# Sums of h moved from GpSimd to the vector engine, and down products two gaps later, in a two-layer attention and feed-forward kernel

## The chip, the cores and the metric

The kernel runs on one core of a Trainium2 chip. TensorE multiplies matrices, VectorE (DVE) and ScalarE (ACT) do elementwise work, GpSimd (POOL) does elementwise work and issues some of the transfers, SyncE (SP) issues the others. Each engine takes its instructions in program order; semaphores tie the engines together. The metric is the device time of the whole program in microseconds, median of several runs. Lower is better.

## What is computed

The input `x` is 16 x 128 x 1024 in f32. The first layer adds to it a cross attention of its layer norm with a context. The second layer, where nearly all the time goes, is a feed-forward block on int4 weights with a scale and a zero for each group of 64:

```
x = x + _L0_xattn_ref(_layernorm(x), ctx_1024, Wq, Wk, Wv, Wskip)
x = x + _L0_ffn_ref(_layernorm(x), ...)
# _L0_ffn_ref:
g = einsum('bsh,ih->bsi', x, Wg);  u = einsum('bsh,ih->bsi', x, Wu)   # 2048 tokens, 1024 -> 2752
h = silu(g) * u
return einsum('bsi,hi->bsh', h, Wd)                                  # 2752 -> 1024
```

Every weight is `(nibble - zero) * scale`.

## The kernel before

**Precision.** f32 data is split in two 16-bit parts, a rounded "hi" (a cast on ACT) and the residual "lo" (a subtraction on DVE). Each product of two blocks is three matmuls: hi·hi, hi·lo, lo·hi.

**Fewer products.** Gate/up and down are each a product of 2 x 2 blocks, done with seven block products instead of eight (the Winograd form of Strassen's scheme). That needs sums of blocks of the weights (S1 to S4), of x (T1 to T4) and, in the down product, of h.

**Tiles.** The 2752 inner features go in 10 pairs (PAIRS) of 256 and a remainder. For each pair there are four `instance`s, one for each half of the pair's features (e = 0, 1) and each half of the tokens (g = 0, 1). Here they are called A (e 0, g 0), B (e 1, g 0), C (e 0, g 1) and D (e 1, g 1). An instance is seven products of 12 matmuls (L569). Their outputs are assembled on DVE in this order: `u1_out`, `u2_out`, `c22_out`, `c21_out`, `c12_out`; ACT does `m1_copy` after the first product, `silu0` after the third, `silu1` after `c12_out`; DVE forms h in `h0_out` (after `c21_out`) and `h1_out` (after `silu1`).

**Groups.** The h of A and B is one group (number 2p for pair p), that of C and D the next (2p+1). Seven blocks of h go into the down product: A11 and A12 (h0 of the first and second instance), A22 (h1 of the second), and four sums, S3 = A11 - A21, S2 = A22 - S3, S1 = A21 + A22, S4 = A12 - S2 (in the code `S3H` etc.). Before the change all four are made on GpSimd: S3 by `last_sum` (L400), S2, S1 and S4 by `first_sums` (L407, L408, L411), one after the other. Each block is then rounded on ACT (`h_block_hi`, L915) and its residual made on DVE (`h_block_lo`, L1396).

**Gaps.** The down product of a group has ten pieces, `down_gap(1)` to `down_gap(10)` (matmuls L607 to L609). TensorE does them in the gaps between the seven products of the two instances that follow: gap 1 after the second product of the first one, gap 2 after the third, and so on to gap 6 after the seventh; gaps 7 to 10 after the first four products of the next. So group 2p-1 is multiplied during A and B of pair p, and group 2p during C and D. Gap 1 needs A11 and A12, and gap 2 begins with a product of S2 and one of S1. ACT scales the results out of PSUM (L918), DVE adds to them (L1399), and GpSimd adds them to `out` in HBM with accumulating transfers: `add11` (L416), `add12` (L422) and `add2` (L429).

**What TensorE waits for in an instance.** The third product needs `m1_copy`; the fourth needs `u1_out` (L1359); the sixth `u2_out` (L1364); the seventh `c22_out`. On DVE `u1_out` stands behind the residuals of S2 and S1.

**Weights.** DVE makes the weights of the next instances in the same stream, in slots `work(0)` to `work(6)` between the steps above: a job is `job_nibbles` (L1249, L1250), `job_minus` (L1254, twice), `times_scale` twice (L1259), residuals (L1264) and sums. A job of gate/up stands in A and B's end for the next e, a job of down weights in B and C. `quant`, `raw` and `grid` are single buffers, so each job's transfers start when the last one is done with them.

**The order of work** is written out by hand in `even_tile` (A and C) and `odd_tile` (B and D), once for ACT and once for DVE. A loop runs over pairs 1 to 9 (here: nine turns); pair 0 stands ahead of it, the last group's down product and the remainder behind it.

## Time and profile before

| | us |
|---|---|
| median of 3 runs | 1476.07 (1474.54 to 1476.49) |
| the profiled execution | 1475.23 |
| its span, first to last instruction | 1473.4 |
| TensorE busy | 1414.7 |
| VectorE busy | 1119.2 |
| ScalarE busy | 678.6 |
| GpSimd busy | 421.3 |

Matmuls overlap in the pipeline: a 128 x 512 one is listed with 0.38 us, but in an unbroken row the next begins 0.216 us later. A row of 12 has 2.75 us in the list, and what follows begins 2.59 us after its start. Where a wait stands in square brackets behind a matmul, the time lost against an unbroken row is that wait and 0.16 to 0.17 us more. VectorE's records overlap a little too: a 128 x 512 operation is listed with 0.68 us, and an independent one can begin 0.60 us after its start, a dependent one 0.72.

### The profile page before, as it was taken

Reading aid. Unit: us, or ns where it says so; the run is one execution under the profiler, and the core shown is the slowest. Engines: PE = TensorE matmul, PEld = TensorE weight load, DVE = VectorE, ACT = ScalarE, POOL = GpSimd, SP = SyncE. Lnnn points to the kernel's source line nnn. Section 1 sums busy time; section 2 is a strip of 40 time slices with the busy share of each in tenths; the row PEclk is TensorE's granted clock in tenths of the full one; section 3 lists DMA queues with packets and bytes.
Section 4 is the critical chain, followed back from the end, with each engine's and each line's share of the span. In section 5 each row is a group of like instructions: output and inputs, shape, how many; then the busy total and the mean of one; then the engine's idle time right before and its main releaser. Section 6 shows DMA issues by size and latency. Waiting matters only on the chain.

```text
span 1473.4 us, 19706 instructions
## 1 busy us (share of the span) xinstructions
PE 1414.7 (96%) x6534; PEld 690.0 (47%) x6534; DVE 1119.2 (76%) x1535; ACT 678.6 (46%) x1269; POOL 421.3 (29%) x425
## 2 busy tenths in 40 slices
PE   8999999899999999999999999999999999999988
PEld 6677764344444444444444444444444444444433
DVE  5898977777778778778778778777778778778565
ACT  6889883334434434444443443443443444444320
POOL 1242322223223323332323323332233233233200
PEclk9999999999999999999999999999999999999999
DMA  5322222276575585675675665764765755756694
GB/s 165 114 85 92 83 86 57 58 143 110 101 146 102 104 142 97 117 125 102 122 121 102 132 121 95 132 117 91 142 113 98 139 107 105 122 115 121 114 322 186
DMA packets 58552, 174.86 MB, mean 119 GB/s; under 512 B 7952, under 2 KB 10768, under 8 KB 54160
## 3 DMA queue, kind: packets, MB, share of 16 engines
q0 software_dynamic: 34560, 83.90, 36.8%
q1 hardware_dynamic: 23808, 90.20, 20.5%
q8 instruction: 20, 0.33, 0.1%
q10 hardware_dynamic: 144, 0.26, 0.1%
q14 instruction: 20, 0.16, 0.0%
HBM read 73.67 MB, written 100.66 MB: 118 GB/s over the span
## 4 chain that ended last, share of the span: by engine, by line
PE 70%; DVE 10%; issue 10%; POOL 5%; ACT 4%; DMA 0%; SPq 0%; DVEq 0%; POOLq 0%
PE ps L569 35%; PE ps L607 8%; PE ps L609 7%; PE ps L608 7%; DVE park L1396 3%; POOL temps L407 3%; PE ps L531 3%; PE ps L498 3%; POOL temps L408 2%; PE ps L756 2%; PE ps L486 1%; PE ps L526 1%; PE ps L520 1%; DVE park L1264 1%; DVE temps L1373 1%
## 5 line engine op out<-in xcount | busy, mean ns | idle before, releaser
L569 PE MATMUL ps<-xt,w_gu 128*128 128x512 f16 x3528 | 798.3, 380 | 2.1 <-DVE temps L1373 2.1
L569 PEld LDWEIGHTS ps<-xt,w_gu 128*128 128x128 f16 x3528 | 345.3, 98 | 420.0 <-DVE temps L1359 5.4
L918 ACT ACTIVATE stage<-ps,pow 128x512 f32<-128x512 f32 x300 | 204.1, 686 | 307.9 <-PE ps L609 306.3
L1399 DVE SCALAR_TENSOR_TENSOR stage<-ps,pow,stage 128x512 f32<-128x512 f32 x220 | 159.5, 747 | 156.0 <-ACT stage L918 87.3
L607 PE MATMUL ps<-park 128*128 128x512 f16 x560 | 212.8, 380 | 35.7 <-DVE park L1396 35.7
L609 PE MATMUL ps<-park 128*128 128x512 f16 x560 | 212.6, 380 | 0.0
L608 PE MATMUL ps<-park 128*128 128x512 f16 x560 | 212.5, 379 | 0.0
L429 POOL DMA_DIRECT2D out<-stage x80 | 69.4, 867 | 288.8 <-ACT stage L918 288.8
L416 POOL DMA_DIRECT2D out<-stage x80 | 70.6, 883 | 276.0 <-DVE stage L1399 276.0
L1396 DVE TENSOR_TENSOR park<-temps,park 128x512 bf16<-128x512 f32 x140 | 125.7, 909 | 20.9 <-ACT park L915 18.1
L915 ACT CAST park<-temps 128x512 f16<-128x512 f32 x140 | 84.2, 615 | 124.2 <-DVE temps L1383 69.9
L607 PEld LDWEIGHTS ps<-park 128*128 128x128 f16 x560 | 54.7, 98 | 116.6 <-DVE park L1396 28.1
L407 POOL TENSOR_TENSOR temps<-temps 128x512 f32<-128x512 f32 x20 | 43.6, 2180 | 217.4 <-DVE temps L1389 217.4
L609 PEld LDWEIGHTS ps<-park 128*128 128x128 bf16 x560 | 54.8, 98 | 66.3 <-issue 0.3
L608 PEld LDWEIGHTS ps<-park 128*128 128x128 f16 x560 | 54.8, 98 | 61.4
L422 POOL DMA_DIRECT2D out<-stage x60 | 68.4, 1140 | 12.1 <-DVE stage L1399 12.1
L498 PE MATMUL ps<-w_gu,park 128*128 128x256 f32 x256 | 62.4, 388 | 1.1 <-ACT w_gu L779 0.5
L794 ACT ACTIVATE temps<-ps,neg_max 128x256 f32<-128x256 f32 x128 | 59.3, 486 | 7.8 <-DVE neg_max L1185 7.5
L531 PE MATMUL ps<-temps,w_gu 128*128 128x512 f32 x128 | 60.2, 593 | 0.6 <-ACT temps L789 0.6
L808 ACT ACTIVATE temps<-temps,inv_total 128x256 f32<-128x256 f32 x128 | 54.7, 504 | 6.9 <-DVE inv_total L1200 6.9
L498 PEld LDWEIGHTS ps<-w_gu,park 128*128 128x128 f32 x256 | 47.6, 193 | 11.7 <-issue 5.3
L1264 DVE TENSOR_TENSOR w_gu<-raw,w_gu 128x1024 f16<-128x1024 f32 (+1 forms) x43 | 53.0, 1232 | 0.0
(123 smaller groups left out, 1715.4 us busy)
## 6 DMA issues: line engine op xcount, KB each, us to landing
out<-stage POOLq DMA_DIRECT2D x80, 512.0 KB, 5.4
out<-stage POOLq DMA_DIRECT2D x140, 256.0 KB, 4.5
grid<-grids SPq DMA_DIRECT2D x136, 256.0 KB, 5.2
raw<-packed SPq DMA_DIRECT2D x34, 512.0 KB, 4.3
out<-stage SPq DMA_DIRECT2D x17, 512.0 KB, 2.7
stage<-x SPq DMA_DIRECT2D x13, 512.0 KB, 3.7
xt<-out SPq DMA_DIRECT2D x12, 512.0 KB, 12.3
out<-xt SPq DMA_DIRECT2D x12, 512.0 KB, 2.7
```

What stands on the lines that cost most here:

```text
L407: pool.tensor_tensor(s3h, u1[:, 1, :], s3h, ALU.subtract).then_inc(s_h_sum, 1)
L416: pool.dma_start(out[t, :, 0:NOUT], stage[:, d % 2, 0:NOUT], accum_op=ALU.add).then_inc(s_add11[d % 2], 16)
L498: mm = pe.matmul(ps_e[f][:, t, :], xn[b % XNS][:, cols], kk[:, par, :], start=True, stop=True)
L531: mm = pe.matmul(ps_o, v_t[:, par, h, :], prob_t[:, f, h, :], start=False, stop=(h == 1))
L569: mm = pe.matmul(bank, w_gu[e][:, wp, w, P * j:P * j + P], xt[:, xb, xp, j, cols], start=(fresh and n == 0), stop=(n == 3 * J - 1), skip_g ...
L607: pe.matmul(bank, h_hi[:, h, rows], w_d[:, 0, w, :], start=fresh, stop=False, skip_group_check=not fresh)
L608: pe.matmul(bank, h_hi[:, h, rows], w_d[:, 1, w, :], start=False, stop=False, skip_group_check=not fresh)
L609: return pe.matmul(bank, h_lo[:, h, rows], w_d[:, 0, w, :], start=False, stop=True, skip_group_check=not fresh)
L915: act.copy(h_hi[:, block, :], src).then_inc(s_h_hi, 1)
L918: return act.activation(dst, ps[:, bank, :], ACT.Copy, scale=pow2[:, 10:11])
L1396: dve.tensor_tensor(h_lo[:, block, :], src, h_hi[:, block, :], ALU.subtract).then_inc(s_h_lo, 1)
L1399: return dve.scalar_tensor_tensor(out=part, in0=ps[:, bank, :], scalar=pow2[:, 10:11], in1=part, op0=ALU.mult, op1=ALU.add)
```

## The change

Four things are changed together.

1. S3, S2 and S4 are made on DVE (`last_sum`, `first_sums_of_h`, `fourth_sum`). S1 stays on GpSimd (`fourth_block`) with a semaphore of its own, and now waits for `h1_out` alone. DVE waits for it ahead of `u1_out`.
2. The down products of the first group of a pair (2p, multiplied during C and D) are shifted by two gaps (`LATER = 2`): gaps 1 to 4 lie after products 4 to 7 of C, gaps 5 to 10 after products 1 to 6 of D. Those of the other group stay.
3. The four C12 parts of a group rotate over three places, so that the next group begins with another place than the last one ended with.
4. Weight work is moved between slots: `times_scale` of `raw` in A goes behind `u1_out`; the last two down weight sums go from B to C, and the residuals of the mixed down weights stand later in C; nibbles and zeros of the next jobs one slot earlier in D and one later in C. On ACT, S4 is rounded after `silu0`.

```diff
+LATER = 2
...
-        part12 = [stage[:, 0, NOUT:N], stage[:, 1, NOUT:N], more[:, :], stage[:, 0, NOUT:N]]
+        places = [stage[:, 0, NOUT:N], stage[:, 1, NOUT:N], more[:, :]]
+        part12 = [[places[(g + k) % 3] for k in range(QUADS)] for g in range(2)]
...
-            def first_sums(group):
-
-                n = 4 * (group // 2) + 2 * (group % 2) + 1
-                pool.wait_ge(s_h1, n + 1)
-                pool.wait_ge(s_h_lo, 7 * group + S3H + 1)
-                pool.tensor_tensor(s3h, u1[:, 1, :], s3h, ALU.subtract).then_inc(s_h_sum, 1)
-                pool.tensor_tensor(s1h, u1[:, 0, :], u1[:, 1, :], ALU.add).then_inc(s_h_sum, 1)
-                pool.wait_ge(s_h_sum, 4 * group + 2)
-                pool.wait_ge(s_h_lo, 7 * group + A12 + 1)
-                pool.tensor_tensor(act_h[:, 1, :], act_h[:, 1, :], s3h, ALU.subtract).then_inc(s_h_sum, 1)
...
+            def fourth_block(group):
+
+                pool.wait_ge(s_h1, 2 * group + 2)
+                wait(pool, s_h_lo, 7 * (group - 1) + S1H + 1)
+                pool.tensor_tensor(s1h, u1[:, 0, :], u1[:, 1, :], ALU.add).then_inc(s_h_sum1, 1)
...
-                instance(4 * p + 2, 0, 1, 0, first_gaps(2 * p, 12 * p + 8))
-                instance(4 * p + 3, 1, 1, 0, last_gaps(2 * p))
+                instance(4 * p + 2, 0, 1, 0, first_gaps(2 * p, LATER, 12 * p + 8))
+                instance(4 * p + 3, 1, 1, 0, last_gaps(2 * p, LATER))
...
+            def last_sum(group):
+
+                dve.wait_ge(s_h1, 2 * group + 1)
+                wait(dve, s_h_lo, 7 * (group - 1) + S2H + 1)
+                dve.tensor_tensor(s3h, act_h[:, 0, :], u1[:, 0, :], ALU.subtract).then_inc(s_h_sum, 1)
+
+            def first_sums_of_h(group):
+
+                dve.wait_ge(s_h1, 2 * group + 2)
+                dve.wait_ge(s_h_lo, 7 * group + S3H + 1)
+                dve.tensor_tensor(s3h, u1[:, 1, :], s3h, ALU.subtract).then_inc(s_h_sum, 1)
+
+            def fourth_sum(group):
+
+                dve.wait_ge(s_h_sum, 3 * group + 2)
+                dve.wait_ge(s_h_lo, 7 * group + A12 + 1)
+                dve.tensor_tensor(act_h[:, 1, :], act_h[:, 1, :], s3h, ALU.subtract).then_inc(s_h_sum, 1)
...
                 before()
+                if group is not None:
+                    first_sums_of_h(group)
                 work(0)
                 if group is not None:
                     h_block_lo(group, S2H)
                     h_block_lo(group, S1H)
+                    dve.wait_ge(s_h_sum1, group + 1)
                 u1_out(n, 0, sums)
```

TensorE, from the last three products of B on, before the change (L569 is an instance's product, L607 to L609 a down product):

```order
L569 MATMUL ps<-xt,w_gu 128x512 x60
...
L607 MATMUL ps<-park 128x512
L608 MATMUL ps<-park 128x512
L609 MATMUL ps<-park 128x512
...
L569 MATMUL ps<-xt,w_gu 128x512 x12
```

and with the change:

```order
L556 MATMUL ps<-xt,w_gu 128x512 x60
L574 REGISTER_ALU
L556 MATMUL ps<-xt,w_gu 128x512 x24
...
L594 MATMUL ps<-park 128x512
L595 MATMUL ps<-park 128x512
L596 MATMUL ps<-park 128x512
```

Before, three products of B and two of C stood in a row (60 matmuls), then gap 1, then one product; now three of B and four of C stand in a row (84), then gap 1.

VectorE at the beginning of the loop, which is the beginning of A, before (L1389 is `h1_out`, L1259 `times_scale`, L1396 the residuals of S2 and S1):

```order
L1389 SCALAR_TENSOR_TENSOR temps<-temps,pow 128x512
...
L1259 SCALAR_TENSOR_TENSOR quant<-quant,pow,grid 128x1024
...
L1259 SCALAR_TENSOR_TENSOR raw<-raw,pow,grid 128x1024
...
L1396 TENSOR_TENSOR park<-temps,park 128x512
```

and with the change (L1414 is `h1_out`, L1458 the sum S2, L1280 `times_scale`, L1421 the residuals, L1384 `u1_out`):

```order
L1414 SCALAR_TENSOR_TENSOR temps<-temps,pow 128x512
...
L1458 TENSOR_TENSOR temps<-temps 128x512
...
L1280 SCALAR_TENSOR_TENSOR quant<-quant,pow,grid 128x1024
...
L1421 TENSOR_TENSOR park<-temps,park 128x512
...
L1384 TENSOR_TENSOR temps<-ps,temps 128x512
```

The sum S2 stands directly behind `h1_out`, and one `times_scale` instead of two stands ahead of the residuals.

VectorE at the end of B, before (L1264 the residuals of the plain down weights, L1297 to L1304 the four down weight sums, L1373 `c21_out`):

```order
L1264 TENSOR_TENSOR park<-raw,park 128x1024
L1297 TENSOR_TENSOR quant<-quant 128x512
L1299 TENSOR_TENSOR quant<-raw,quant 128x512
L1302 TENSOR_TENSOR raw<-raw,quant 128x512
...
L1304 TENSOR_TENSOR raw<-raw 128x512
L1373 TENSOR_TENSOR temps<-ps,temps 128x512
```

and with the change (L1285, L1398 `c21_out`, L1408 `h0_out`, L1319 and L1321 the first two sums, L1402 `c12_out`):

```order
L1285 TENSOR_TENSOR park<-raw,park 128x1024
L1398 TENSOR_TENSOR temps<-ps,temps 128x512
L1408 SCALAR_TENSOR_TENSOR temps<-temps,pow 128x512
...
L1421 TENSOR_TENSOR park<-temps,park 128x512
L1319 TENSOR_TENSOR quant<-quant 128x512
L1321 TENSOR_TENSOR quant<-raw,quant 128x512
L1402 TENSOR_TENSOR temps<-ps,temps 128x512
```

`c21_out` no longer stands behind four sums, and two of them stand between it and `c12_out`; the other two are in C.

## Rows read from the trace of the kernel before

**Rows 1.** The page: span, busy time and share, instructions of each engine.
```profile
span 1473.4 us, 19706 instructions
PE 1414.7 (96%) x6534; PEld 690.0 (47%) x6534; DVE 1119.2 (76%) x1535; ACT 678.6 (46%) x1269; POOL 421.3 (29%) x425
```
**Rows 2.** TensorE's waits, whole span: who waited for whom, us, times, longest.
```profile
PE ps L607 <- DVE park L1396: 35.7, 40, 1.8
PE ps L569 <- DVE temps L1373: 2.1, 1, 2.1
```
**Rows 3.** The same for the nine loop turns alone, 327 to 1345 us.
```profile
PE ps L607 <- DVE park L1396: 31.6, 36, 1.8
```
**Rows 4.** TensorE in time, around gap 2 of A: start, duration, [idle before].
```profile
771.51 13.11 PE L569 MATMUL ps<-xt,w_gu 128*128 128x512 f16 x60
785.76 2.75 PE L569 MATMUL ps<-xt,w_gu 128*128 128x512 f16 x12
790.20 0.39 PE L607 MATMUL ps<-park 128*128 128x512 f16 x1 [1.68 <-DVE park L1396]
791.80 0.39 PE L607 MATMUL ps<-park 128*128 128x512 f16 x1 [0.78 <-DVE park L1396]
```
**Rows 5.** TensorE in time, around gap 2 of C.
```profile
828.72 13.11 PE L569 MATMUL ps<-xt,w_gu 128*128 128x512 f16 x60
846.04 0.39 PE L607 MATMUL ps<-park 128*128 128x512 f16 x1 [0.33 <-DVE park L1396]
847.55 0.39 PE L607 MATMUL ps<-park 128*128 128x512 f16 x1 [0.69 <-DVE park L1396]
```
**Rows 6.** VectorE and GpSimd in time, beginning of A.
```profile
783.11 1.22 DVE L1254 TENSOR_TENSOR raw<-raw,grid 128x1024 f32<-128x1024 int32 x1
784.91 1.28 DVE L1259 SCALAR_TENSOR_TENSOR quant<-quant,pow,grid 128x1024 f32<-128x1024 f32 x1
785.08 2.23 POOL L407 TENSOR_TENSOR temps<-temps 128x512 f32<-128x512 f32 x1 [9.94 <-DVE temps L1389]
786.11 2.29 DVE L1259 SCALAR_TENSOR_TENSOR raw<-raw,pow,grid 128x1024 f32<-128x1024 f32 x1
787.28 2.23 POOL L408 TENSOR_TENSOR temps<-temps 128x512 f32<-128x512 f32 x1
788.32 1.75 DVE L1396 TENSOR_TENSOR park<-temps,park 128x512 bf16<-128x512 f32 x1
```
**Rows 7.** VectorE, GpSimd and ScalarE in time, end of B and beginning of C.
```profile
833.85 0.69 DVE L1297 TENSOR_TENSOR quant<-quant 128x512 f32<-128x512 f32 x1
838.69 0.68 DVE L1377 TENSOR_TENSOR temps<-ps,temps 128x512 f32<-128x512 f32 x1
839.41 0.72 ACT L898 ACTIVATE temps<-temps,pow 128x512 f32<-128x512 f32 x1 [0.59 <-DVE temps L1377]
841.02 0.75 DVE L1389 SCALAR_TENSOR_TENSOR temps<-temps,pow 128x512 f32<-128x512 f32 x1
844.01 1.26 POOL L408 TENSOR_TENSOR temps<-temps 128x512 f32<-128x512 f32 x1
844.07 0.62 ACT L915 CAST park<-temps 128x512 f16<-128x512 f32 x1 [0.78 <-POOL temps L407]
847.41 0.68 DVE L1359 TENSOR_TENSOR temps<-ps,temps 128x512 f32<-128x512 f32 x1
```
**Rows 8.** Busy time of each engine in one loop turn: stretch, length, PE, PEld, DVE, ACT, POOL, clock.
```profile
779.20:892.30 113.10, 109.62 (x507) 49.02 (x505) 86.92 (x108) 47.24 (x70) 35.09 (x32) 1.00 0.64 116
```
**Rows 9.** TensorE in time, first pair: gap 2 of the first group.
```profile
281.21 0.61 PE L607 MATMUL ps<-park 128*128 128x512 f16 x1 [0.85 <-DVE park L1396]
282.47 3.71 PE L569 MATMUL ps<-xt,w_gu 128*128 128x512 f16 x12
```
**Rows 10.** Line L297, the load of `raw`: issue to landing, all 34.
```profile
DMA to landing us min/median/max: 3.1/4.3/6.7
```
**Rows 11.** TensorE in time, the loop's one product at a lower clock.
```profile
1018.44 4.36 PE L569 MATMUL ps<-xt,w_gu 128*128 128x512 f16 x12
```

312 lines of the change are left out of this document (173 added, 139 removed).

## The prediction

> **What bounds the kernel now.** First the page: TensorE is busy for 1414.7 of 1473.4 us [rows 1], so nothing can be won but its pauses, unless matmuls are removed, and none is. Then its waits: 35.7 us stand in 40 waits at one line, L607, the down products, for the residuals of h (L1396) [rows 2]; 36 of these waits, 31.6 us, are in the nine loop turns [rows 3]. Then the timeline of one turn: all four waits stand in gap 2, ahead of the product of S2 and that of S1, two in A and two in C [rows 4, 5]. A row of 60 matmuls takes 60 x 0.216 = 12.95 us, a row of twelve 2.59. In A, the product at 785.76 ends a row at 788.35, and the next matmul starts at 790.20: 1.85 us lost, where the view says 1.68. A wait costs 0.17 more than it is listed with. The nine turns lose 31.6 + 36 x 0.17 = 37.7 us, about 2.8 in each A and 1.35 in each C.
>
> Why is gap 2 late in A? GpSimd's sum S2 (L407) and VectorE's `times_scale` alternate: L407 takes 2.23, the second `times_scale` 2.29 where the first took 1.28, L408 2.23, and the residual of S2 1.75 instead of 0.68 [rows 6]. With VectorE idle GpSimd needs 1.26 for the same sum [rows 7]. Each of them waits for the other to end. The Trainium skill says the same of it ("SBUF — State Buffer", section "Who interferes with whom"): a VectorE instruction with two SBUF inputs and a GpSimd instruction that reads SBUF exclude one another, and the first to issue holds the port for the whole instruction. By that rule the trace agrees: 1.26 us of work took up to 2.23.
>
> **The change, part by part.** *C, the shifted group.* I follow the new order with the durations of the rows, on the clock of [rows 5, 7]. B's seventh product ends at 828.72 + 36 x 0.216 = 836.49; call this T. Gap 2 of C now lies after the fifth product, at T + 14.2 (five products of 2.59 and gap 1 of 6 x 0.216), and the residuals of S2 and S1, which came at T + 9.4 and T + 10.9 [rows 5], are far ahead of it. These two waits go: 1.35 a turn. But gaps 1 and 2 covered something: the fourth product waits for `u1_out`, which stands behind both residuals. It used to be wanted at T + 10.36, and now, with no gap ahead of it, at T + 7.77. So what is late next is `u1_out`, and the chain to it has to be walked.
> - VectorE is free at 833.85, where the four down weight sums began [rows 7]. `c21_out` takes their place at 834.10 (the sixth product ends at 833.90, and a result is read 0.2 later), then `h0_out`, the residual of S3 and two sums: 0.72 + 0.67 + 0.60 + 0.72 + 0.61, so `c12_out` starts at 837.42, T + 0.9. It was 838.69 [rows 7].
> - ScalarE rounds the first mixed down weights from 837.53, 0.95 us, then `silu1` 838.48 to 839.20 (0.72 [rows 7]). `h1_out` 839.23 to 839.97. It was 841.02.
> - Sum S2 on VectorE, priced by L1297 of the same shape, 0.69 [rows 7]: to 840.67. GpSimd sees `h1_out` 0.09 later, so it finds the port taken and does S1 from 840.67 to 841.93, at its 1.26. ScalarE rounds S2 (0.62) to 841.32 and S1 to 842.59; the residual of S2 waits for GpSimd and ends at 842.5, that of S1 at 843.28.
> - `u1_out` follows 0.60 after the start of that residual, 843.20 to 843.88, and TensorE starts 0.13 later (788.32 + 1.75 to 790.20 [rows 4, 6]): 844.01. It is wanted at 844.26. Slack 0.25 us.
>
> That is thin. The loop's two-register waits on VectorE and ScalarE may cost 0.05 to 0.1 each in such a chain, so the new wait lies between 0 and 0.4 us; I take 0.1, since the walk ends ahead of time: +1.0 in nine turns.
>
> *A, the group that stays.* D's end is T'. VectorE there: `nibbles` now before `c21_out`, then `h0_out`, residual S3, an add, two `job_minus` of 1.13 (listed 1.22 [rows 6]), so `c12_out` at T' + 1.3; `silu1` to T' + 2.8, `h1_out` to 3.6, sum S2 to 4.3. In between, what stood ahead of `h1_out`, 2.3 us of `job_minus`, is gone. GpSimd's S1 runs 4.3 to 5.55, `times_scale` waits and runs to 6.65. ScalarE first scales gap 1's result, ready at T' + 5.83, until 6.6, then rounds S2 to 7.2; residual 8.0, seen at 8.1. It is wanted at 9.07. S1: 8.7 against 9.72. `u1_out`: 9.3 against 10.36. All two waits go, 2.8 us a turn, with 1 us to spare.
>
> *What else moves.* VectorE gains three sums a group, 6 x 0.69 = 4.1 us a turn, on 86.9 of 113.1 [rows 8]: 91 of 109, still 84%. They cost nothing as long as nobody waits behind them: in A the fourth sum and the `times_scale` moved behind `u1_out` delay `u2_out` to T' + 15.9, wanted at 20.1. In C two down weight sums, their residuals and the fourth sum end at T + 13; mixed down weights are wanted at 14.2, `u2_out` (13.5) at 15.5. GpSimd loses 3 of 4 sums, and its transfers, which stand behind the sums, start no later. The C12 places: each is written again at least three parts later; even at 7 us a transfer the place is free; nothing. Rounding S4 after `silu0`: S4 is wanted in gap 4; nothing.
>
> *The load of `raw` in C* is the other narrow place. It can be issued at T + 13.1, and VectorE waits for it in `nibbles`, ahead of `c21_out`, `h0_out` and the add whose result the last product of gap 4 needs at T + 24.6. With the median landing of 4.3 [rows 10] that add ends at T + 23.2: slack 1.35 us, so landings up to 5.65 cost nothing.
>
> *Outside the loop.* There are 35.7 - 31.6 = 4.1 us in four waits, 0.7 more by their 0.17, 2.3 for the first C's wait for `c21_out` (2.1 [rows 2]), and 1.6 at half clock behind the first one (3.71 against 2.75, 0.61 against 0.38 and the five matmuls between [rows 9]): 8.7. `c21_out` loses the four sums ahead of it, 2.8 us, so its wait goes. But the first pair's VectorE runs late, and without gap 1 as cover `m1_copy` and `u1_out` hold TensorE there for some 1.5 + 1.65 us. Won: 8.7 - 3.2 = 5.5, between 3 and 8.7.
>
> *The clock.* The other product at a lower clock (4.36 against 2.75 [rows 11]) stands right behind the two waits of an A. With these gone I take its 1.6 us as gone.
>
> **Sum.** -37.7 + 1.0 - 5.5 - 1.6 = -43.8 us. The profiled execution took 1475.2, 0.8 under the median: 1476.1 - 43.8 = 1432.3, say 1432.5. If every pause named here vanished: 37.7 + 8.7 + 1.6 = 48, 1428.
>
> **The rivals.**
> - *GpSimd first.* S1 on GpSimd and S2 on VectorE are released by the same `h1_out`. If GpSimd takes the port first, the sum starts 1.26 later, `u1_out` in C is seen at 844.6 instead of 844.0, and TensorE waits 0.35 us; with late registers up to 1.2. In nine turns +3 to +11, less the 1.0 already in the sum: 1435 to 1443. Against it: `h1_out` to the next VectorE operation is 0, to GpSimd 0.09 (841.02 + 0.75, and [rows 6] has L407 at 785.08). The skill's SBUF page (section "SBUF: two separate sides") has the rule that whoever starts first holds the port for the whole instruction; by it this rival's wait is the whole 1.26 or nothing. Chance 20%.
> - *The raw load lands late.* The longest seen is 6.7 [rows 10]: 1.05 us a turn, +9: 1442. Against it: in C it is issued before GpSimd's first transfer of the group. 6%.
> - *The chain in C stays as long as it is.* From the start of `h1_out` to the end of `u1_out` 841.02 to 848.09 [rows 7], 7.07 us. Then `u1_out` is seen at 846.4, 2.2 late, +19: 1451. 8%.
> - *A's waits stay in part* (S2 ready, but held behind something on ScalarE): half of 25 us stays, 1445 to 1458. 5%.
> - *Slower.* The `raw` load in C, 512 KB, would have to land more than 5.65 + 4.2 = 9.9 us after its issue: then the new wait is larger than the 4.15 us that a turn gains. At 12 us a turn loses 2.1, nine lose 19, and with the 6 won outside it ends at 1489. No landing over 6.7 is in the trace, but VectorE's stream is fuller than before and other transfers move under it. 3%.
> - *Nothing gained*: the waits only change their line, 1476. 2%.
>
> **How the numbers follow.** The forecast (1428 to 1436) has 56%, GpSimd first 20%, late load 6%: these give 1428 to 1443. To have 8 in 10 with some room for the chain in C, the range is 1427 to 1447. Within 0.2% (3 us, about what a measurement of this kernel can tell from no change) 3%, slower 4%, faster 93%.
>
> **What would show it.** Right: no wait at a down product in A or C beyond the first pair; the period of a turn 108.9 to 109.3 us instead of 113.1; VectorE's S2 sum ending about 0.7 after `h1_out`, GpSimd's S1 at 1.3 to 2.0. Wrong at the chain in C: a wait of an L556 product on `u1_out` in every C. Wrong at the load: `nibbles` in C waiting for the transfer over 3 us and a down product waiting for L1424. Wrong at the lock: VectorE's sum listed with about 1.9 us.

## The result, and the profile after

| | median us | ratio to before | 95% interval |
|---|---|---|---|
| before | 1476.28 (1474.54 to 1476.49, 4 runs) | | |
| after | 1425.69 (1425.62 to 1425.75, 4 runs) | 0.966 | 0.9643 to 0.9677 |

The change gains 50.6 us. The forecast was 43.8, and its range (1427 to 1447) begins 1.3 us above the result: the direction came as told, the size did not. The waits that were named went, but not all for the reasons given, as the experiments show. The profiled execution of after took 1425.65 us, span 1423.8, so between the two profiled executions there are 49.6 us.

The page of after, span and TensorE, answers to [rows 1]:

```profile
span 1423.8 us, 19828 instructions
PE 1402.8 (99%) x6534; PEld 692.5 (49%) x6534; DVE 1121.7 (79%) x1595; ACT 682.3 (48%) x1269; POOL 312.8 (22%) x365
```

TensorE's waits over the whole span, those outside the attention part (who waited <- for whom: us, times, longest), answer to [rows 2]:

```profile
PE ps L507 <- DVE xt L1211: 4.2, 4, 1.8
PE ps L556 <- DVE temps L1384: 1.4, 1, 1.4
PE ps L556 <- ACT temps L874: 1.3, 1, 1.3
PE ps L743 <- DVE xt L1736: 1.2, 2, 1.0
```

The 40 waits at the down products, 35.7 us, are gone: L594, the first matmul of a down product (L607 before), has no row here. The two L556 rows are in C of the first pair; L507 are transposes, 3.7 of the 4.2 us in A and B of the first pair; L743 is in the remainder behind the loop.

One loop turn of after (stretch, length, busy time and instructions of PE, PEld, DVE, ACT, POOL, granted clock, DMA share, GB/s) answers to [rows 8]:

```profile
1023.64:1132.42 108.78, 108.78 (x506) 49.31 (x504) 87.20 (x114) 47.66 (x71) 24.14 (x26) 1.00 0.66 121
```

A turn is 108.78 us instead of 113.10, and TensorE is busy for all of it. VectorE works 87.20 us in it, where 86.92 were before, although three sums a group were added. Those are 4.1 us, but VectorE's other instructions are held up less by GpSimd's sums: a residual of h (L1421, L1396 before) is listed with 709 ns on average instead of 909, 2.8 us for the 14 of a turn. GpSimd falls from 35.09 to 24.14.

The chain in C, in the turn whose T (end of B's seventh product, start of C's first) is 1140.03: VectorE, GpSimd and ScalarE in time (start, duration), which answer to [rows 7]:

```profile
1140.97 0.69 DVE L1402 TENSOR_TENSOR temps<-ps,temps 128x512 f32<-128x512 f32 x1
1142.79 0.75 DVE L1414 SCALAR_TENSOR_TENSOR temps<-temps,pow 128x512 f32<-128x512 f32 x1 [0.54 <-ACT temps L884]
1143.57 0.69 DVE L1458 TENSOR_TENSOR temps<-temps 128x512 f32<-128x512 f32 x1
1143.62 1.76 POOL L431 TENSOR_TENSOR temps<-temps 128x512 f32<-128x512 f32 x1 [8.73 <-DVE temps L1414]
1145.42 1.14 ACT L904 CAST park<-temps 128x512 f16<-128x512 f32 x2 [0.51 <-POOL temps L431]
1144.95 1.82 DVE L1421 TENSOR_TENSOR park<-temps,park 128x512 bf16<-128x512 f32 x2 [0.68 <-ACT park L904]
1146.68 0.68 DVE L1384 TENSOR_TENSOR temps<-ps,temps 128x512 f32<-128x512 f32 x1
```

`c12_out` starts at T + 0.94 (forecast 0.9), `h1_out` at T + 2.76, the sum S2 (L1458) takes 0.69, and GpSimd's S1 (L431), released by the same `h1_out`, starts 0.05 behind it, is listed with 1.76 and ends at T + 5.35. `u1_out` (L1384) ends at T + 7.33. With the 0.13 of a semaphore TensorE could go on at T + 7.46, and it wants to at T + 7.77: 0.31 us of room. The forecast had 0.25.

In A the two sums come in the other order. Here is the A behind that C, whose start T' is 1194.42:

```profile
1197.20 0.75 DVE L1414 SCALAR_TENSOR_TENSOR temps<-temps,pow 128x512 f32<-128x512 f32 x1 [0.19 <-ACT temps L884]
1198.08 1.76 DVE L1458 TENSOR_TENSOR temps<-temps 128x512 f32<-128x512 f32 x1
1198.04 1.26 POOL L431 TENSOR_TENSOR temps<-temps 128x512 f32<-128x512 f32 x1 [3.23 <-DVE temps L1414]
```

GpSimd starts 0.04 us ahead, and VectorE's sum is listed with 1.76 instead of 0.69. It is so in A of all nine loop turns; in the other eleven of the 20 groups VectorE is first. A has room for it: no TensorE wait follows.

**Where the 49.6 us are.** Split the program where the 84 matmuls of the remainder start. Before they start at 1402.14, after at 1357.59: 44.55 us are won up to there. Of these 39.5 are in the nine loop turns (1018.5 us before, 979.0 after, by the starts of TensorE's matmuls), 3.3 ahead of the loop and 1.8 between the loop and the remainder. From the remainder's first matmul to the end of the span it was 71.25 us and is 66.26: another 5.0 us, in a part whose order of work the diff leaves as it was. The forecast of 43.8 is nearly exact for the first part, and had nothing for the second. The experiments begin there.

### The profile page after: what moved, and what is told of

The parts are those of the page before. It is cut to its first block, busy times and chain, and to the rows that moved or that the text cites. A ratio compares the mean times of both kernels' runs of the same rounds, so it can differ in the third digit from the quotient of the medians.

```text
span 1423.8 us, 19828 instructions
## 1 busy us (share of the span) xinstructions
PE 1402.8 (99%) x6534; PEld 692.5 (49%) x6534; DVE 1121.7 (79%) x1595; ACT 682.3 (48%) x1269; POOL 312.8 (22%) x365
## 4 chain that ended last, share of the span: by engine, by line
PE 89%; DVE 5%; ACT 3%; issue 2%; DMA 0%; POOL 0%; SPq 0%; DVEq 0%; POOLq 0%; ACTq 0%
PE ps L556 50%; PE ps L596 8%; PE ps L595 8%; PE ps L594 8%; PE ps L518 3%; PE ps L485 3%; PE ps L743 2%; PE ps L473 1%; PE ps L513 1%; PE ps L507 1%; ACT temps L781 1%; ACT temps L795 1%; PE ps L723 1%; DVE neg_max L1206 0%; DVE w_gu L1285 0%
## 5 line engine op out<-in xcount | busy, mean ns | idle before, releaser
L556 PE MATMUL ps<-xt,w_gu 128*128 128x512 f16 x3528 | 795.9, 379 | 2.7 <-DVE temps L1384 1.4
L556 PEld LDWEIGHTS ps<-xt,w_gu 128*128 128x128 f16 x3528 | 345.1, 98 | 417.9 <-DVE temps L1384 1.9
L594 PE MATMUL ps<-park 128*128 128x512 f16 x560 | 212.2, 379 | 0.0
L904 ACT CAST park<-temps 128x512 f16<-128x512 f32 x140 | 83.1, 614 | 64.8 <-DVE temps L1408 38.1
L1421 DVE TENSOR_TENSOR park<-temps,park 128x512 bf16<-128x512 f32 x140 | 98.4, 709 | 17.0 <-ACT park L904 13.9
L595 PEld LDWEIGHTS ps<-park 128*128 128x128 f16 x560 | 54.8, 98 | 66.1
L594 PEld LDWEIGHTS ps<-park 128*128 128x128 f16 x560 | 54.8, 98 | 66.1
L596 PEld LDWEIGHTS ps<-park 128*128 128x128 bf16 x560 | 54.8, 98 | 66.1
L408 POOL DMA_DIRECT2D out<-stage x60 | 66.9, 1115 | 6.6 <-DVE stage L1424 6.3
L431 POOL TENSOR_TENSOR temps<-temps 128x512 f32<-128x512 f32 x20 | 30.7, 1535 | 150.0 <-DVE temps L1414 150.0
L1285 DVE TENSOR_TENSOR w_gu<-raw,w_gu 128x1024 f16<-128x1024 f32 (+1 forms) x43 | 53.1, 1235 | 7.7 <-ACT w_gu L844 6.1
```

Source lines behind the costliest of these rows:

```text
L556: mm = pe.matmul(bank, w_gu[e][:, wp, w, P * j:P * j + P], xt[:, xb, xp, j, cols], start=(fresh and n == 0), stop=(n == 3 * J - 1), skip_g ...
L594: pe.matmul(bank, h_hi[:, h, rows], w_d[:, 0, w, :], start=fresh, stop=False, skip_group_check=not fresh)
L595: pe.matmul(bank, h_hi[:, h, rows], w_d[:, 1, w, :], start=False, stop=False, skip_group_check=not fresh)
L596: return pe.matmul(bank, h_lo[:, h, rows], w_d[:, 0, w, :], start=False, stop=True, skip_group_check=not fresh)
L904: act.copy(h_hi[:, block, :], src).then_inc(s_h_hi, 1)
L1421: dve.tensor_tensor(h_lo[:, block, :], src, h_hi[:, block, :], ALU.subtract).then_inc(s_h_lo, 1)
```

## The experiments

The second column is the median. The other three are of the profiled execution: the nine loop turns, the start of the remainder's first matmul, and the time from there to the end of the span.

| kernel | us | nine turns | start of the remainder | remainder |
|---|---|---|---|---|
| before | 1476.3 | 1018.5 | 1402.1 | 71.3 |
| `x_act5`: before + 5 small ScalarE copies | 1470.12 | 1018.3 | 1400.6 | 66.9 |
| `x_dve5`: before + 5 small VectorE memsets | 1478.85 | 1020.3 | 1402.8 | 73.3 |
| `x_sums`: before + sums on VectorE | 1453.61 | 1005.8 | 1385.5 | 66.0 |
| `y_pool`: after, sums on GpSimd | 1444.92 | 989.9 | 1369.9 | 72.5 |
| `y_pool_act5`: that + 5 ScalarE copies | 1439.35 | 989.9 | 1371.2 | 66.0 |
| `y_order`: after, old order of the down weights | 1463.37 | 1013.3 | 1397.2 | 66.2 |
| `y_late1`: after, shift of one gap | 1467.06 | 1014.3 | 1399.7 | 66.1 |
| `y_scale`: after, both scales ahead of `u1_out` in A | 1425.53 | 979.0 | 1357.6 | 66.1 |
| `y_dup2`: after, 1.2 us more ahead of `u1_out` in C | 1434.74 | 987.1 | 1368.9 | 65.4 |
| `y_s1dve`: after, S1 on VectorE too | 1424.53 | 979.0 | 1357.3 | 65.4 |
| `y_first2`: after, first pair reordered | 1424.60 | 979.0 | 1357.5 | 66.4 |
| `y_best`: both, and more of the first pair | 1421.01 | 979.0 | 1353.4 | 66.0 |
| after | 1425.69 | 979.0 | 1357.6 | 66.3 |

### Five instructions that do nothing

In the remainder of before, ScalarE and TensorE in time. `y_silu` is L1099; in square brackets stands the idle time before the instruction and what ended it:

```profile
1420.03 0.62 ACT L1106 CAST park<-temps 64x512 f16<-64x512 f32 x1
1424.59 0.68 ACT L1099 ACTIVATE temps<-ps,pow 64x512 f32<-64x512 f32 x1 [3.94 <-issue]
1426.89 0.82 PE L756 MATMUL ps<-park,w_gu 128*128 128x512 f16 x3 [4.30 <-DVE xt L1678]
1428.10 1.49 PE L756 MATMUL ps<-park,w_gu 128*128 128x512 f16 x3
```

"issue" says that ScalarE waited for no semaphore. Behind it stands the longest wait of TensorE outside the attention part, 4.30 us, and then matmuls at a lower granted clock (a row of three takes 1.49 instead of 0.82). The same place in after:

```profile
1376.11 0.62 ACT L1127 CAST park<-temps 64x512 f16<-64x512 f32 x1
1376.63 0.68 ACT L1120 ACTIVATE temps<-ps,pow 64x512 f32<-64x512 f32 x1
1379.07 0.82 PE L743 MATMUL ps<-park,w_gu 128*128 128x512 f16 x3 [1.03 <-DVE xt L1736]
```

The third `y_silu` follows at once, TensorE waits 3.27 us less, and no slow matmuls come behind. Counted by the records of the trace, with the loop's body counted once, the third `y_silu` is ScalarE's 832nd of 840 before and the 838th of 846 after, since the rearranged gaps write a few more. (The recorded expectation below counts otherwise, and has 626 and 630.) So the first theory is that a place in ScalarE's instruction stream pauses, not a piece of work. `x_act5` is before with

```
+            for k in range(5):
+                act.copy(total[:, k // 4, k % 4:k % 4 + 1], pow2[:, k:k + 1])
             act.wait_ge(s_down3, 2 * QUADS * PAIRS)
             act.wait_ge(s_weight, 6 * PAIRS + 5)
```

> The kernel before with five one-column ScalarE copies (into unused columns of `total`) added in the remainder, at a place where ScalarE waits 5.78 us anyway, and nothing else. What is tested: in the kernel before, ScalarE stands 3.94 us with no releaser ahead of the third `y_silu` (instruction 626 of its program, counting each copy of a row that order prints as xN), TensorE then waits 4.30 us at 1426.89, and in the kernel after both are gone (the same instruction is number 630 there). Theory A (the pause belongs to a place in ScalarE's instruction stream, where new instructions are fetched, on a DMA queue that row loads fill at that moment): the pause moves to another instruction, up to five earlier in the remainder's work, TensorE's wait of 4.30 shrinks to about 1, and the time falls by 3 to 5 us, to 1471 to 1473; if it lands on a copy that feeds the y chain earlier, a smaller wait of its own is left. Theory B (the pause belongs to the moment or to what the third `y_silu` waits for, such as a semaphore from VectorE or the loads of the rows): it stays at the third `y_silu`, with TensorE's 4.3 us, and the time stays within 1 us of 1476.3.

1470.12 us (1469.32 to 1471.83) against 1476.35 on the same chip, ratio 0.9956 (0.9939 to 0.9972): 6.2 us faster through five instructions that compute nothing, 0.9 us more than the expected range allowed. ScalarE and TensorE in its remainder:

```profile
1412.22 0.62 ACT L1107 CAST park<-temps 64x512 f16<-64x512 f32 x1 [5.01 <-DVE temps L1636]
1420.25 0.68 ACT L1101 ACTIVATE temps<-ps,pow 64x512 f32<-64x512 f32 x1
1422.68 0.82 PE L756 MATMUL ps<-park,w_gu 128*128 128x512 f16 x3 [1.59 <-DVE xt L1680]
```

The pause is gone from the third `y_silu`, TensorE's wait is 1.59 us instead of 4.30, and the matmuls behind run at full clock. The DMA view tells where the pause went. It lists packets of a queue q14 of kind "instruction" (packets, MB, share of 16 engines); first before, in 1420.7 to 1424.6, ScalarE's pause:

```profile
q14 instruction: 1, 0.01, 0.5%
```

then `x_act5`, in 1407.0 to 1412.2, where ScalarE waits 5.01 us for VectorE in any case:

```profile
q14 instruction: 2, 0.02, 0.8%
```

The packet in the pause starts at 1422.94, and another follows 4.83 us later; the two of `x_act5` start at 1407.02 and 1411.84, 4.82 apart. The view doesn't say for which engine a packet is, so that these are ScalarE's is read from their places and distances, not shown. The remainder is 4.4 us shorter; the other 1.5 to 1.8 us of the 6.2 lie ahead of it, within the spread of before (1474.3 to 1479.6), and I do not assign them.

`x_dve5` is the control: the same number of instructions, on VectorE.

```
+            for k in range(5):
+                dve.memset(inv_total[:, k // 4, k % 4:k % 4 + 1], 0.0)
             dve.memset(park[HALF:P, 1792:2816], 0.0)
```

> The kernel before with five one-column VectorE memsets (into unused columns of `inv_total`) added in the remainder, ahead of the memset of `park`, and nothing else; ScalarE's program is untouched. Theory A (a place in ScalarE's own stream): ScalarE's 3.94 us ahead of the third `y_silu` stay, TensorE waits 4.3 us, time 1476 within 1 us. Theory A' (two engines' fetches collide on one queue, VectorE's at about 1420.5 and ScalarE's at 1423): moving VectorE's by five instructions parts them, the pause falls to about half, the time by about 2 us. Theory B (the moment, not the stream): as A.

1478.85 (10 runs), ratio 1.0015 (1.0005 to 1.0025): 2.5 us slower. ScalarE's pause stays at its third `y_silu`, at 3.94 us to the digit:

```profile
1427.62 0.68 ACT L1099 ACTIVATE temps<-ps,pow 64x512 f32<-64x512 f32 x1 [3.94 <-issue]
1416.13 0.69 DVE L1628 TENSOR_TENSOR w_gu<-temps,w_gu 128x512 bf16<-128x512 f32 x1 [1.93 <-issue]
```

That "no change" was expected and not found has its reason in the second row: VectorE now has a pause of its own, 1.93 us, and it stands in the chain of `y`: TensorE waits 5.9 us there instead of 4.3. A q14 packet starts at 1414.21, with the pause; before, the one in its place starts at 1415.44, while VectorE works. So five instructions moved VectorE's pause into the chain and left ScalarE's alone. The theory of colliding fetches falls: ScalarE's pause did not shrink.

The same was tried once more on another kernel, `y_pool` (below), which has the pause (3.85 us) and TensorE's wait (4.60):

> The kernel after with the three sums back on GpSimd, and the five one-column ScalarE copies in the remainder as well. Alone, the sums on GpSimd gave 1444.9 and a pause of ScalarE of 3.85 us ahead of the third `y_silu`, with TensorE's wait of 4.6 us behind it, as in the kernel before. Theory A (a place in ScalarE's stream): the pause leaves that spot here too, 1438.5 to 1441. Theory B (what the remainder's timing is): 1444.9 within 1 us.

1439.35 (1437.36 to 1442.77) instead of 1444.92, the remainder 6.4 us shorter, and TensorE's wait there:

```profile
1392.45 0.82 PE L761 MATMUL ps<-park,w_gu 128*128 128x512 f16 x3 [0.78 <-DVE xt L1730]
```

Over all kernels: the three whose ScalarE program has 840 records (before, `x_dve5`, `y_pool`) pause at the third `y_silu`, 3.85 to 3.94 us; the eleven with 845 or 846 don't. That the diff made this stream six records longer is therefore the reading that fits all fourteen kernels; `x_act5`, which changes nothing else, wins 4.4 of the 5.0 us. VectorE's stream is 30 records longer by the same count, and in after it pauses 3.75 us ahead of the last `u2_out`, where nobody waits for it.

The Trainium skill ("Runtime: NRT & Kernel Launch", section "Instruction fetch mechanics") has the mechanism: each engine's stream is fetched block by block over a DMA queue while the block before is executed, strictly in sequence, a branch out of the loaded blocks stalls, and crossing a block's border is "mostly hidden". The trace agrees with a border at a place in the stream and differs in the last point: behind the loop the pause was not hidden, with 3.2 to 4.1 us. That a border between blocks, and not the way out of the loop, is what costs here is not shown. Pauses of nearly one length stand beside different loads of the DMA engines: 3.94 us (ScalarE) in before with a DMA share of 1.02 in 1420.6 to 1424.6, 3.75 us (VectorE) in after with 0.55 in 1347.6 to 1351.4.

### Sums alone, and all the rest alone

`x_sums` is before with the three sums of after on VectorE, and S1 alone on GpSimd:

```
             def even_tile(n, group, before, sums, work):
                 before()
+                first_sums_of_h(group)
                 work(0)
                 ...
                 u1_out(n, 0, sums)
                 down_gap(group, 1)
+                fourth_sum(group)
             def odd_tile(n, group, own, before, sums, work):
                 ...
                 down_gap(group, 7)
+                last_sum(own)
                 work(0)
```

`y_pool` is the counterpart, after with GpSimd's `last_sum` and `first_sums` of before put back and VectorE's taken out (GpSimd's part):

```
             for group in range(2 * PAIRS):
-                fourth_block(group)
-                for at in range(1, 11):
+                first_sums(group)
+                cut = 8 if group % 2 else 6
+                for at in range(1, cut):
                     adds(group, at)
+                if group + 1 < 2 * PAIRS:
+                    last_sum(group + 1)
+                for at in range(cut, 11):
+                    adds(group, at)
```

> The kernel before with only the three sums (S3, S2, S4) moved from GpSimd to VectorE; down products, places of C12 and weights work stay as they were. My theory (the down products in C start before their inputs are there, so the shift by two gaps is what removes most of the wait; the sums themselves only shorten the chain): after h1_out VectorE makes the S2 sum in 0.69 us instead of GpSimd's 1.26 to 2.2, and GpSimd starts S1 at the same moment, so that the chain to `u1_out` is about 1.3 us shorter in C and in A, and the waits fall by about that: 1.3 us in A and in C in each of the nine turns, 20 to 25 us in all, time 1451 to 1456, turn about 110.5. Rival (GpSimd's sums were the whole chain, the shift and the weight order bring nothing more): almost the whole gain, 1430 or less. Second rival (VectorE's queue is full there, the sums push back the scales of the weights and the down products' results): under 8 us of gain, 1468 or more, with the waits now released by VectorE's L1259 or L1262 work.

> The kernel after with the three sums put back on GpSimd (shift by two gaps, three places for C12 and order of the weights work stay). My theory: in A, GpSimd needs S2, S1 and S4 in a row, its S1 ends 2 to 2.5 us later than now, and `u1_out` is late by that less the slack; in C the slack is 0.47 us, so 1.5 to 2 us of wait come back there; S4's is hidden in C by the shift and late in A. Together 2.5 to 4 us a turn in nine turns: time 1448 to 1462, turn 111.3 to 112.8. Rival (the shift did it all): within 3 us of 1425.7.

`x_sums`: 1453.61 (1453.33 to 1454.28), ratio 0.9842 (0.9825 to 0.9858). The time is in the expected range, but by luck: the turn is 111.75 where 110.5 was expected, the nine turns win 12.7 us instead of 20 to 25, and 5.2 us are the remainder's, whose pause is gone (its ScalarE program has 846 records). TensorE's waits in it, at the down products (L590):

```profile
PE ps L590 <- ACT stage L904: 14.7, 10, 1.6
PE ps L590 <- DVE park L1382: 8.6, 10, 1.3
```

One of each is in C of the first pair, the other nine of each are in A. In C of the loop no wait is left, though nothing is shifted here. One A, TensorE and ScalarE:

```profile
782.29 0.39 PE L590 MATMUL ps<-park 128*128 128x512 f16 x1 [0.81 <-DVE park L1382]
787.96 0.39 PE L590 MATMUL ps<-park 128*128 128x512 f16 x1 [1.61 <-ACT stage L904]
784.65 0.62 ACT L901 CAST park<-temps 128x512 f16<-128x512 f32 x1 [3.79 <-DVE temps L1425]
787.23 0.68 ACT L904 ACTIVATE stage<-ps,pow 128x512 f32<-128x512 f32 x1
```

ScalarE stands 3.79 us for the sum S4 (L1425) ahead of `silu0` and of the scaling of gap 2's result (L904), and TensorE waits 1.61 us for that scaling. In after ScalarE rounds S4 behind both.

`y_pool`: 1444.92 (1444.17 to 1446.47), ratio 0.9785 (0.9768 to 0.9801), 3 us under the expected range, although 6 us of it are the remainder's pause. Its waits:

```profile
PE ps L574 <- DVE temps L1399: 12.3, 10, 2.9
PE ps L761 <- DVE xt L1728: 4.8, 2, 4.6
```

I expected waits in A and in C. All ten at L574 are in C, at `u1_out`, about 1.04 in a loop turn; in A the chain has room for GpSimd's sums too. Up to the start of the remainder the sums alone give 16.7 us, shift, places and order alone 32.2, and all together 44.55: nearly the sum, less 4.3.

Side by side, the waits of TensorE in one loop turn (view's us, in A and in C): before 2.5 and 1.0, `x_sums` 2.4 and 0, `y_pool` 0 and 1.04, after 0 and 0. So C is cleared by the sums on VectorE, and A by the rest of the change. In that rest the shift can't be A's cure, since it touches only the other group; what is left is the order of work on VectorE and ScalarE and the places, which no run takes apart further than `y_scale` below.

### The order of the down weights

`y_order` is after with

```
             def down_weights(p):                       # VectorE
                 if at == 4:
                     down_plain_lo(3 * p + 2)
-                if at == 5:
                     down_first_sums(3 * p + 2)
+                    down_second_sums(3 * p + 2)
+                if at == 6:
+                    down_mixed_lo(3 * p + 2, 0)
             def next_weights(p):
-                if at == 1:
-                    down_second_sums(3 * p + 2)
-                    down_mixed_lo(3 * p + 2, 0)
-                if at == 2:
+                if at == 0:
                     down_mixed_lo(3 * p + 2, 1)
```

and ScalarE's two roundings back in B.

> The kernel after with the down weights' work of B and C back in its old order (all four sums behind the plain low halves in B, the first mixed low half at B's end, the second ahead of `u1_out` in C); the sums of h on VectorE, the shift and the places of C12 stay. My theory (that work stood in the chain of C): 1.22 us of mixed low half come in ahead of `h1_out` and 1.22 ahead of the residuals; the second is half hidden under VectorE's 0.69 of waiting for ScalarE there and the 0.47 of room, so `u1_out` ends 0.3 to 0.8 us behind TensorE's want: 3 to 7 us in nine turns and 1 to 2 in the first pair, 1430 to 1434. Rival (the room takes it all): 1425.7 within 1 us. Rival (it is as costly as its busy time): 2.4 us less 0.47 in ten instances, 1445.

1463.37 (1461.32 to 1466.10), ratio 0.9912 (0.9882 to 0.9941): 37.7 us slower than after, and 9.8 slower than the sums alone. TensorE and VectorE in C, T = 1058.87:

```profile
1059.08 0.68 DVE L1396 TENSOR_TENSOR temps<-ps,temps 128x512 f32<-128x512 f32 x1
1061.07 0.69 DVE L1400 TENSOR_TENSOR temps<-ps,temps 128x512 f32<-128x512 f32 x1
1064.79 2.29 DVE L1283 TENSOR_TENSOR park<-raw,park 128x1024 f16<-128x1024 f32 x1
1068.21 0.68 DVE L1382 TENSOR_TENSOR temps<-ps,temps 128x512 f32<-128x512 f32 x1
1068.95 4.03 PE L556 MATMUL ps<-xt,w_gu 128*128 128x512 f16 x12 [2.15 <-DVE temps L1382]
```

I had mis-added the chain. The four sums stand ahead of `c21_out`, which comes at T + 0.21 instead of T - 2.39, so `c12_out` comes at T + 2.2 as in before, and not at T + 0.94 as in after. And the mixed low half ahead of the residuals meets GpSimd's S1 and is listed with 2.29 instead of 1.22. TensorE waits 2.15 us. The second cost is in the duration: twelve matmuls in 4.03 us instead of 2.75, with this granted clock (third figure from the end; a stretch in the form of the turn above):

```profile
1068.90:1072.70 3.80, 3.75 (x12) 1.47 (x13) 1.88 (x3) 0.62 (x1) 0.00 (x0) 0.68 0.25 98
```

0.68 on average, between the levels of 1.2 and 2.4 GHz. In eight of the nine turns the twelve matmuls behind the 2.15 were slow, in one (at 957.85) they took 2.76, at a granted clock of 1.00. L556 is busy 811.9 us in all, in after 795.9: 16 us more, beside 22.4 us more of waits. So the shift needs the order of the down weights: without it, after is 9.8 us slower than the sums alone, with it 27.9 faster.

But these 27.9 are not the shift's. `x_sums` has no wait in C that a shift could take away; 26.7 of them are in the nine turns, where what `x_sums` still loses is A's two waits. No run has the sums on VectorE and the new order in A without the shift, so what the shift itself brings stays open. What is shown is what it costs when the chain in front of `u1_out` stays long: with it `u1_out` is wanted at T + 7.77 instead of T + 10.36.

### One gap instead of two

`y_late1` is after with

```
-LATER = 2
+LATER = 1
```

> The kernel after with the first group's down products one gap later than in the kernel before instead of two (`LATER = 1`), everything else kept. My theory (what sets the two gaps is the second half of the down weights, whose low part VectorE makes in C behind `u1_out`): the chain to `u1_out` is as now, but the down product with T2D stands at T + 11.7 instead of T + 14.1, while VectorE's last low half of the down weights ends at T + 12.7 in the trace of after and 0.74 later here, because the first result of the down products is added ahead of it: a wait of 1.5 to 2 us in C, released by VectorE's L1285, in ten instances, 1440 to 1446. Rival (one gap is enough, the second is not used): 1425.7 within 2 us.

1467.06 (1466.68 to 1467.54), ratio 0.9938 (0.9922 to 0.9955), 41.4 slower than after. Its waits at the down products:

```profile
PE ps L594 <- DVE park L1285: 24.0, 10, 3.9
PE ps L594 <- DVE park L1421: 4.6, 6, 1.1
```

The wait was the expected one, for the low half of the mixed down weights (L1285), 2.25 in a loop turn where 1.5 to 2 was expected. The time was 21 us over the expected range for two reasons that I had left out: 4.6 us of waits at the residuals of h (L1421), which I did not trace further, and 12.6 us of matmuls at a lower granted clock behind the waits (L556 busy 800.4 instead of 795.9, the three lines of a down product 2.6 to 2.9 us more each). Of the nine waits of 2.24 us in C, five were followed by slow matmuls and four by a row at full clock.

### How much room there is

`y_scale` undoes the split of the scales in A; `y_dup2` puts 1.2 us of VectorE work (two subtractions into unused memory) ahead of `u1_out` in C.

```
                     if at == 0:                        # y_scale, second_up
                         times_scale(q, 6 * p + 3, 6)
-                    if at == 1:
                         times_scale(r, 6 * p + 4, 6)
```

```
                     dve.wait_ge(s_h_sum1, group + 1)   # y_dup2, even_tile
+                    if late:
+                        extra_lo()
                 u1_out(n, 0, sums)
```

> The kernel after with one thing undone: in A, VectorE multiplies both halves of the weights by their scale ahead of `u1_out` again, instead of one half ahead and one behind. My theory (a chain with room): in the kernel after, VectorE stands 0.71 us ahead of the residuals of S2 and S1 (waiting for ScalarE's rounding of S2) and `u1_out` ends 1.1 us before TensorE's product wants it (1203.66 against 1204.78 in the last turns), so that 1.2 more is taken up by the 0.71 and the rest by the room: 1425.7 within 1 us, no wait of TensorE in A. Rival (the order of the weights work is what removes A's waits): at least 0.6 us of wait comes back in each of ten instances A, 6 to 12 us, 1432 to 1438.

> The kernel after with two VectorE subtractions of 64x448 into unused memory added in C between the residual of S1 and `u1_out` (about 0.6 us each, ten groups). What is tested is how much room the chain in C has: by the trace `u1_out` ends at T + 7.17 and is wanted at T + 7.77 less the 0.13 a semaphore takes, 0.47 us of room. My theory: 1.2 us less 0.47 = 0.73 us of wait in C in each of nine turns and 1.2 in the first pair, which has no room: 7.8 us in all, 1433.5 (1431 to 1436), turn 109.5, TensorE waiting for L1384 or its neighbour `u1_out`. Rival (the chain in C is not on the path, other work covers it): under 2 us. Rival (what follows `u1_out` in VectorE's queue is as tight, such as `fourth_sum` and the residual of S4): 10 us or more, waits at down products as well.

`y_scale`: 1425.53 (1425.52 to 1425.55), after 1425.69: no wait in A came back, that part of the order is worth nothing. `y_dup2`: 1434.74 (1434.32 to 1436.14), expected 1433.5. The wait in a loop turn is listed with 0.73:

```profile
1048.49 2.76 PE L558 MATMUL ps<-xt,w_gu 128*128 128x512 f16 x12 [0.73 <-DVE temps L1386]
```

The turn is 109.68 us, 0.90 longer than in after, and `u1_out` ends at T + 8.60, 1.27 later. So the room is 0.37 us, near the 0.31 that the rows of after give. That 0.73 was expected to the digit is luck: the 0.47 of room behind it took T 0.16 us too late, and a wait costs 0.17 more than it is listed with. The product behind it takes 2.76: no lower clock after 0.73 us, nor after the 1.04 of `y_pool`.

### A faster version

`y_s1dve` moves the last sum:

```
-                fourth_block(group)                    # GpSimd
                     first_sums_of_h(group)             # VectorE, even_tile
+                    s1_sum(group)
```

`y_first2` changes VectorE's `first_tile` and `next_weights` (ScalarE's `plain_hi(2, 1)` goes from gap 2 to 3):

```
+                if at < 4:
+                    block_lo(LATE[at])
                 if at == 0:
                     job_nibbles(1)
-                    block_lo(LATE[0])
-                    job_minus(1)
                 if at == 1:
-                    block_lo(LATE[1])
-                    job_scale(1, 6)
-                if at in (2, 3):
-                    block_lo(LATE[at])
+                    dve.wait_ge(s_grid_in, 16 * QG * 2)
+                    minus_zero(q_int, 3)
+                if at == 2:
+                    minus_zero(r_int, 4)
+                    times_scale(q, 3, 6)
                 if at == 3:
+                    times_scale(r, 4, 6)
                     plain_lo(1, 4)
...
                     if at == 1:                        # next_weights
+                        if isinstance(p, int):
+                            down_first_sums(3 * p + 2)
                         down_second_sums(3 * p + 2)
```

`y_best` has both, and

```
                         if isinstance(p, int):         # next_weights
+                            down_plain_lo(3 * p + 2)
                             down_first_sums(3 * p + 2)
+            def end_and_block():                       # before() of instance 1
+                block_lo(LATE[4])
+                end_of(0, 0)()
```

with `plain_lo(1, 4)` one gap later, and the same `end_and_block` with `block_hi` on ScalarE.

> The kernel after with the fourth sum S1 on VectorE too, behind S2; GpSimd computes nothing for h any more and only issues adds. My theory (in C the chain to `u1_out` goes through GpSimd's S1, which takes 1.76 us beside VectorE's work instead of 1.26, and ends at T + 5.2; on VectorE it would end at T + 4.8): `u1_out` comes 0.2 to 0.3 us earlier in C, no wait comes back, time 1425.7 within 1 us; VectorE is busy 14 us longer. Rival (VectorE's queue has no room for 0.7 us more in each of the twenty groups, so GpSimd has to keep a part): waits of 0.3 to 0.7 us in each group, 1431 to 1439.

> The kernel after with the first pair's weights work moved: the first sums of the down weights go from B into C behind `u1_out`, where they stand in no other pair, and in the first instance VectorE makes each transposed block's low half ahead of the weights work of that gap instead of behind it (ScalarE's rounding of those weights goes one block later). My theory: the two waits of TensorE in C of the first pair (1.30 and 1.38 us) go, and of the waits at the transposes (1.75, 1.60, 0.35) some 1.7 us go until the low halves of the second instance's weights set the pace: 1425.7 - 2.7 - 1.7 = 1421.3 (1420 to 1423.5). Rival (the weights of the second instance come later and take it back): 1424 to 1428, with a new wait at the first products of the second instance.

> The kernel after with S1 on VectorE (alone 1424.53), the first pair's order of weights and transposed blocks (alone 1424.60), and two more edits in the first pair: the low halves of the plain down weights go into C as well, behind `u1_out`, and the fifth late block's halves are made ahead of `silu1` and `h1_out` in the second instance. My theory: what is left of TensorE's waits in the first pair (1.38 at `u1_out` in C, 1.61 and 0.65 at the transposes, 1.26 at `c22_out`) shrinks by 3 to 4 us in all beyond what the two gave: 1420 to 1422.5. Rival (VectorE's queue in the first pair is full, the work moved into C comes back as waits at the first down products): 1423 to 1427.

`y_s1dve`, S1 on VectorE and nothing for h on GpSimd: 1424.53 (1424.41 to 1424.67), 1.2 us faster than after, just outside the 1 us that I allowed. The nine turns take the same 979.0 us. In the first pair `u1_out` is waited for 0.86 instead of 1.38, of which 0.25 us reach the start of the remainder; 0.84 us are won in the remainder, which I did not trace.

`y_first2` gave 1424.60 (1424.18 to 1425.68), 1.1 us where 4.4 was expected, a miss. The 1.30 of `m1_copy` went, but the 1.38 at `u1_out` stayed, since `c12_out` was still 3.3 us behind T (VectorE's low halves of the down weights stand in front of it), and 1.3 us of wait came new at `c22_out` (L1394), behind the second instance's weights. Hence the further edits of `y_best`.

`y_best`: 1421.01 us (1420.39 to 1421.42), ratio to before 0.9626 (0.9610 to 0.9642), 4.7 us or 0.33% faster than after. TensorE's waits in its first pair are 2.2 us, where after has 6.4:

```profile
PE ps L587 <- DVE park L1282: 1.1, 1, 1.1
PE ps L500 <- DVE xt L1208: 0.6, 1, 0.6
PE ps L549 <- DVE w_gu L1282: 0.5, 1, 0.5
```

## Why the prediction was right where it was, and where it failed

- **What bounds the kernel, and the waits of the loop: right.** The sum had -37.7 + 1.0 for nine turns and -1.6 for the slow product, -38.3. Found were 39.5 (1018.5 to 979.0).
- **The walk through C: right within 0.1 us.** `c12_out` was forecast at T + 0.9 and came at T + 0.94; `u1_out` was to be seen by TensorE at T + 7.5, and was at T + 7.46. The +1.0 of new waits did not come: the 0.31 us of room held in every turn. `y_dup2` shows that the room is real, and `y_order` that the chain it belongs to is the one that decides.
- **A: right in time, not in its course.** No wait is left there; `u1_out` ends at T' + 9.24 (forecast 9.3) and is wanted at T' + 10.36. `y_pool` and `y_scale` show that A would have borne more.
- **What cures C: wrong.** The forecast wrote C's 1.35 us a turn to the shift. In `x_sums`, without a shift, they are gone as well, and in `y_pool`, with the shift and the sums on GpSimd, 1.04 stand at `u1_out`. It is the sums on VectorE that clear C. The total did not suffer, since both were changed.
- **Outside the loop, up to the remainder: -5.5 forecast, 5.1 found** (3.3 ahead of the loop, 1.8 behind). The new waits in C of the first pair were forecast with 1.5 and 1.65; they are listed with 1.30 and 1.38 (273.41 and 277.55), 1.47 and 1.55 with the 0.17 of each.
- **The load of `raw` in C: no trouble,** as forecast. `nibbles` waited for it 1.37 us and started at T + 16.5; issue and landing in the forecast add up to T + 17.4.
- **GpSimd first: it happened, but in A.** In C, which the forecast priced, VectorE's S2 sum came first in every turn. In A of all nine turns GpSimd's S1 came first, and VectorE's sum was listed with 1.76, the forecast's own sign for "wrong at the lock". It cost nothing, for A has about 1 us to spare. What the same order would have cost in C, with 0.31 us of room, no run shows.
- **The step that failed is the sum's frame.** "TensorE is busy for 1414.7 of 1473.4 us [rows 1], so nothing can be won but its pauses", the prediction says, and then it prices the pauses of the loop and of the first and last group only. In the view of [rows 2] there is also

```profile
PE ps L756 <- DVE xt L1678: 4.5, 2, 4.3
```

  which is the remainder's wait, and slow matmuls behind it. I took the remainder as untouched, because the diff does not touch its order of work, and gave it no term. It gave 5.0 us. "If every pause named here vanished, 1428" was no bound for that reason: the result is 2.3 us below it. `x_act5` wins 4.4 us in the remainder with neither sums, shift nor weights changed.
- **The account.** 43.8 forecast, 5.0 from the remainder, 1.2 more in the loop, 0.4 less ahead of and behind it, and 1.0 by which the median of before lies above its profiled execution: 50.6.
- **A price that the forecast never stated.** It took the order of the down weights as part of the walk through C, without a term of its own. With the shift in place that order is worth 37.7 us (`y_order`). This is not a part of the 50.6: `x_sums` has neither shift nor new order, and no wait in C.

## What to carry to other kernels

A shift makes other waits come earlier: what was covered by the shifted work is wanted sooner. Walk the chain to the operation that is wanted next, and price the order of the fill-in work in front of it; here, with the shift in place, the old order cost 37.7 us, and the room left by the new one is a third of a microsecond. When several things are changed together, ask of each stage which of them cures it, and run each alone: here the stage that the shift was meant for was cured by the sums. When a kernel is bound by TensorE, make the list of its waits complete over the whole span and give each one a line in the sum, also those in parts that the diff leaves alone; a wait behind an engine with idle time "issue" can go or come with an edit that changes the number of that engine's instructions. And a wait of 2 us can cost more than itself.

## What the runs showed of the hardware

- An engine can pause 3.2 to 4.1 us with no semaphore behind it (ScalarE 3.94 and 3.85; VectorE 3.75 in after, 3.42 in `x_sums`, 4.09 in `y_first2`, 3.21 in `y_best`; 1.93 in `x_dve5`), at a place that moves with its instruction stream. Five one-column copies moved one such pause off the critical path: the remainder got 4.4 us shorter in one kernel and 6.4 in another (medians 6.2 and 5.6). Five memsets moved one onto it, for 2.5.
- TensorE's clock behind a wait: after 0.73 and 1.04 us the next twelve matmuls took 2.76; after 2.15 they took 4.03 in the turn shown, at a granted clock of 0.68 in that stretch, and 2.76 in another turn of the same run. The length of the wait alone doesn't tell.
- Of a VectorE and a GpSimd sum released by the same semaphore, either can come first: in after VectorE's in eleven of 20 groups, GpSimd's in nine, always those of A in the loop. The later one is listed longer: GpSimd's with 1.76 instead of 1.26, VectorE's with 1.76 instead of 0.69. In `y_order` a VectorE subtraction that came upon a running S1 was listed with 2.29 instead of 1.22.
